# Two semaphore thresholds in the tap loop of a state-space convolution kernel, each set one block later

## The reference, cut to what matters

```python
# batch 8, sequence 2048, d_model 512, state 64
A_bar = jnp.exp(DT * A)                        # A = -exp(log_A), 512 x 64
B_bar = (A_bar - 1.0) / A * B_param
t = jnp.arange(seq_len)
powers = jnp.exp(jnp.log(A_bar)[:, :, None] * t)
K = jnp.einsum('dn,dnl->dl', C * B_bar, powers)   # the taps
...                                               # y = causal convolution of layernorm(x) with K
y = y + D[:, None] * x_t
x = x + y                                         # then the attention on layernorm(x)
```

## Time and profile before

| what | value |
|---|---|
| median of 3 runs | 4608.75 us (4600.84 to 4609.76) |
| the profiled execution's own time | 4609.76 us |
| its span in the trace | 4608.0 us |
| PE, DVE, ACT, POOL busy | 92%, 63%, 41%, 19% of the span |
| end of the first phase | 142.9 us |

### The profile page before, as it was taken

The page is one execution under the profiler, slowest core; times in us unless marked ns, Lnnn a source line. Parts: engine busy times, 40 slices in busy tenths (PEclk is TensorE's granted clock), DMA queues, the critical chain, the costliest instruction groups (busy, mean ns, idle before and its releaser), DMA issues. The chain is left out here.

```text
span 4608.0 us, 94516 instructions
## 1 busy us (share of the span) xinstructions
PE 4222.1 (92%) x37156; PEld 3543.2 (77%) x37156; DVE 2911.6 (63%) x4980; ACT 1869.2 (41%) x4842; POOL 897.4 (19%) x678
## 2 busy tenths in 40 slices
PE   9687848999999999999999999649999999999998
PEld 9577737888888888878888888437877778777777
DVE  7777737767667667665555666585564654646545
ACT  6333313434433434434444433234353443544434
POOL 0222201222222222222222222310101101111011
PEclk9988869999999999999999999859999999999999
DMA  8888552222222222212121221210202202012010
GB/s 306 205 219 225 150 156 83 85 88 85 83 88 82 85 89 84 76 56 65 57 65 60 62 64 46 88 46 12 51 8 51 45 15 52 12 48 45 15 42 13
DMA packets 341163, 369.21 MB, mean 80 GB/s; under 512 B 22896, under 2 KB 220784, under 8 KB 340720
## 3 DMA queue, kind: packets, MB, share of 16 engines
q1 hardware_dynamic: 262384, 295.91, 21.7%
q0 software_dynamic: 12288, 33.56, 3.5%
q10 hardware_dynamic: 66048, 33.56, 2.7%
HBM read 236.60 MB, written 76.02 MB: 68 GB/s over the span
## 5 line engine op out<-in xcount | busy, mean ns | idle before, releaser
L1503 POOL TENSOR_TENSOR l_prob<-l_prob,l_inv 128x768 f32<-128x768 f32 x256 | 389.3, 1542 | 1692.7 <-DVE l_inv L1462 1692.7
L1155 ACT ACTIVATE l_prob<-l_ps_s,l_neg_max 128x192 f32<-128x192 f32 x1024 | 420.7, 444 | 2.3 <-DVE l_neg_max L1438 2.1
L2213 DVE TENSOR_REDUCE h_neg_max<-h_ps_s 128x1 f32<-128x1024 f32 x256 | 312.8, 1222 | 166.8 <-PE h_ps_s L1999 163.7
L2134 ACT ACTIVATE h_prob<-h_ps_s,h_neg_max 128x1024 f32<-128x1024 f32 x256 | 285.5, 1115 | 292.5 <-DVE h_neg_max L2216 292.5
L1438 DVE TENSOR_REDUCE l_neg_max<-l_ps_s 128x4 f32<-128x768 f32 x256 | 233.1, 952 | 245.6 <-PE l_ps_s L963 226.2
L2011 PE MATMUL h_ps_t<-ident,h_prob 128*128 128x128 f32 x2048 | 272.8, 276 | 14.4 <-ACT h_prob L2134 13.9
L2011 PEld LDWEIGHTS h_ps_t<-ident,h_prob 128*128 128x128 f32 x2048 | 228.1, 140 | 62.7 <-issue 27.7
L2023 PEld LDWEIGHTS h_ps_o<-h_probs_t,h_val 128*64 128x64 f32 x4096 | 220.9, 137 | 43.1 <-issue 36.9
L2023 PE MATMUL h_ps_o<-h_probs_t,h_val 128*64 128x128 f32 x4096 | 251.9, 276 | 0.0
L2270 DVE COPY h_probs_t<-h_ps_t 128x512 f32<-128x512 f32 x256 | 176.8, 691 | 116.0 <-PE h_ps_t L2011 114.4
L1155 ACT ACTIVATION_READ_ACCUMULATOR l_prob<-l_ps_s,l_neg_max 128x1 f32 x1024 | 236.5, 231 | 0.0
(11 more groups left out here) (388 smaller groups left out, 11273.0 us busy)
## 6 DMA issues: line engine op xcount, KB each, us to landing
xin<-in_L_attn_x_dram SPq DMA_DIRECT2D x32, 1024.0 KB, 5.2
xg<-in_L_attn_x_dram SPq DMA_DIRECT2D x64, 512.0 KB, 9.6
toep_back<-taps_padded ACTq DMA_DIRECT2D x32, 1024.0 KB, 7.1
x<-xg SPq DMA_DIRECT2D x64, 512.0 KB, 7.3
l_xin<-x SPq DMA_DIRECT2D x128, 256.0 KB, 3.3
l_xres<-x SPq DMA_DIRECT2D x128, 256.0 KB, 3.1
l_val_side<-l_val SPq DMA_DIRECT2D x256, 128.0 KB, 3.1
out_dram<-l_res SPq DMA_DIRECT2D x128, 256.0 KB, 2.1
```

Of the source, the lines that this page charges most:

```text
L1155: last = nc.scalar.activation(prob[t % 2][:, h, pair, :], ps_s[:, h, pair, BOTH], ACT.Exp, bias=neg_max[:, t % 2, h, pair:pair + 1], accum ...
L1503: nc.gpsimd.tensor_tensor(mine, mine, spread(inv[:, t % 2, h, :], [1, PAIRS], [0, WIN + P]), ALU.mult).then_inc(p_normed, 1)
L2134: nc.scalar.activation(prob[i % 2][:, :].rearrange("p (a k) -> p a k", a=2), ps_s[i % 2][:, :, :], ACT.Exp, bias=neg_max[:, qt % 2, h:h + ...
L2213: nc.vector.tensor_reduce(at, ps_s[i % 2][:, :, :].rearrange("p a k -> p (a k)"), AX_X, ALU.max, negate=True).then_inc(max_step, 1)
```

## The change

Two thresholds change in the tap loop. PE's wait for `taps_kept` before block k (k = s2 * 2 + par) asks for k copied blocks, where it asked for k - 1. ACT's wait for `taps_made` before block k asks for `s2 * 2` blocks, where it asked for k - 1: for an even k that is k (one more than before), for an odd k it is k - 1 (as before). Buffers, instructions and their order are the same.

```diff
                 def taps_of_two(s2):
                     for par in range(2):
                         pe.wait_ge(powers_made, s2 * 2 + par + 1)
-                        wait(pe, taps_kept, s2 * 2 + par - 1)
+                        wait(pe, taps_kept, s2 * 2 + par)
                         for q in range(SPAIRS):
                             last = nc.tensor.matmul(ps_taps[par][:, 2 * q:2 * q + 2], powers[par][:, q, :],
...
                 def powers_of_two(s2):
                     for par in range(2):
-                        wait(act, taps_made, s2 * 2 + par - 1)
+                        wait(act, taps_made, s2 * 2)
                         for q in range(SPAIRS):
                             last = nc.scalar.activation(
```

## The result

The changed kernel takes 4654.6 us (median of 4 runs, 4651.1 to 4659.5) against 4604.8 us (4600.0 to 4609.8) of the kernel before: a ratio of 1.0109, with a 95% interval of 1.0092 to 1.0127. That is slower by about 50 us. Its profiled execution took 4653.88 us, with a span of 4652.2 us.

The account below looks back on a forecast made before the run. PE was taken to bound the tap loop, with SP's queue of loads behind it. The last copy's +53.8 us, less 7.7 hidden and half of at most 1.2, gave +45.5 us: 4654 us, range 4642 to 4664.

Parts of the forecast that it names:

- The pair of blocks: Tap loop: an even block of 6.32 us plus an odd one of 4.05, 10.37 us where it was 6.83.
- The handover: Tap loop: time from a finished awaited block to the start of waiting PE, taken as 0.15 us, bounds 0.05 and 0.25.
- The last copy: End of the tap loop: last block's copy at 174.6 us instead of 120.81, +53.8 us (bounds +50.7 and +56.9).
- What is given back: Behind the tap loop: 7.7 us of its loss hidden by `xg` loads starting earlier against the loop's end, leaving +46.1 us.
- The further 0.6 us: SP's queue: fewer loads in flight when `xg` starts win at most 1.2 us; half taken, +46.1 to +45.5 us.
- the 0.36 MB: SP's queue: extra loads still queued when `xg` started in the kernel before, 1.3 us at 288 GB/s.
- One to one to the end: Later phases: they start from the same state, so the first phase's shift passes whole to the kernel's end, +45.5 us.
- a changed length of the later phases: Phases behind the first: if their length changed, the prediction was to count as wrong; no size given.
- The clock: Tap loop: PE already runs at its lower level, 1.2 GHz, despite the column's 1.00, and loses nothing by new gaps.
- The rival of a falling clock: Tap loop: gaps take PE from 2.4 to 1.2 GHz, 3.41 us more a block, 4762 us in all; chance 0.04.
- The free result buffer: Odd blocks of the tap loop: PE's wait for the copy costs nothing, 3.41 not 4.05 us, 4646 us; chance 0.05.
- The rising clock: Tap loop: PE's clock goes up, blocks of 2.00 us, pairs of 6.91, about 4608 us, no change; chance 0.02.

Follow-up runs that it names:

- the hold of the loads: Loads of `xg` held until all 128 tiles have statistics: kernel before, phase end 154.60 us, whole 4612.6 us; changed kernel, 209.91 us and 4672.5 us.
- The warm-up: Kernel before with twelve full-precision products of 512 columns of x ahead of the tap loop, result unused: phase end 152.25 us, whole 4615.7 us.

## Why the prediction was right

The forecast was 4654 us, measured 4654.6. The closeness to 1 us is chance. The median before moved from 4608.75 to 4604.8 with one more run, and the shift of the medians is 49.8 us where 45.5 was forecast; its interval, 1.0092 to 1.0127, is 42 to 58 us. What was worked out, the shift of the phase's end, came to 47.3 us, inside the bounds of +42.3 and +48.7. Point by point:

- **The pair of blocks.** 10.37 us foretold, 10.46 measured. ACT's 2.44, the copy's 0.17 and PE's 3.73 from a start held. The handover was taken as 0.15 (0.05 to 0.25): 0.15 behind ACT, 0.26 behind the copy, of which 0.15 is the loop's own work by the run with the loop written out.
- **The last copy.** 174.6 foretold, 175.88 measured, +55.1 for +53.8. The difference is 15 pairs of 0.09.
- **What is given back.** 7.7 us foretold, 7.8 measured, and the hold of the loads showed that it comes from SP's queue. `xg` began at 153.89 (152.9 foretold), `krow` was written at 182.90 (181.9), the next phase began at 190.21 (189.0). The further 0.6 us, taken for loads that are no longer in flight, did not come: the loads took 28.96 us as before. No row gives the 0.36 MB on which that term rests.
- **One to one to the end.** Not contradicted: +49.7 at the end of the second phase, +44.2 in the span, against 47.3 at the phase's end; the differences are within what unchanged code varies by from trace to trace. For the same reason a changed length of the later phases, named as a sign of being wrong, could not have served as one at this size, and the runs' spread of 9 us was taken too small (18.6 us in 13 runs).
- **The clock.** That the column's 1.00 in the first 160 us is not to be believed, and that the loop runs at the lower level already, was argued from line 517's two durations. The warm-up showed it. The rival of a falling clock is out for this kernel. With the rule that a waiting matrix engine drops to its lower clock (the Trainium skill, "TensorE: Matmul & The Clock Gate", Part 1), the trace with 128 columns and the new waits agrees, with 0.50 to 0.67 in its later windows, where the same products without the new waits kept to 2.05 us a block.
- **The free result buffer.** Out: PE's threshold alone costs 20.2 us. The same page of the Trainium skill, in "HAM oscillation — how this bites in real kernels", reports a kernel in which double-buffering of the result banks gave nothing further; that does not carry over to this loop, in which PE sets the pace.
- **The rising clock.** The changed kernel does not show it, as said. But the price put on it was about right for a level that stays up: the block of 2.00 us from its start is what the first block behind the warm-up took, and against pairs of 6.9 the first such pair with 128 columns took 7.4. It also named a lever that the widened products then pulled in the kernel before.

## What to carry to other kernels

A wait that asks for the block just made turns two buffers into one; its price is the neighbour's work plus the restart of the pacing engine, and it can be summed from one timeline before it is tried. Follow the loss to the end of the phase: what queues behind the loop (here 29 us of loads and then a write of 7.1) decides how much is given back. And check a clock column against the spacing of equal instructions at two places; where an engine is "busy" at its lower level, making its products wider than needed can be faster, as it was here with 128 columns and was not with 64.

## What was not expected of the hardware

- Products of 2 or of 64 moving columns kept PE at 213 ns a record for some 109 us without a gap; 128 columns, with the same weight loads, ran at 128 ns from the third block on, and the whole kernel was 0.39% faster (0.9961, 0.9946 to 0.9975).
- The clock column read 1.00 in runs in which the spacing was that of 0.50, until its first change. After one, it agreed with the spacing.
- The write of `krow` (0.5 MB) held the phase for 3.8 us when it was issued 6 us behind the last load, and for 7.1 to 8.2 us directly behind 16 transfers; the 16 transfers themselves took from 26.8 to 31.7 us.
